# Cross-attention and mixture-of-experts block on one Trainium2 core: nine phases of two score slots in place of six of three, and the row maxima of two slots taken off in one pass

## The reference, cut to what matters

```python
q = latents @ Wq                       # latents = the 1024 rows of x, 8 heads of 64
k, v = split(concat([ctx, latents]) @ Wkv)
q = l2norm(q) * q_scale
k = l2norm(k) * k_scale
sim = einsum('bhid,bhjd->bhij', q, k) * 8
sim = where(mask, sim, -max)
attn = softmax(sim)                    # in float32
out = einsum('bhij,bhjd->bhid', attn, v)
x = x + layer_norm(out @ Wo)
x = x + shared_expert(ln(x)) + top2_of_16_experts(ln(x))
```

## Time and profile before

| | us |
|---|---|
| median of 3 runs | 801.37 (801.15 to 801.73) |
| the profiled execution, its own time | 803.27 |
| span of its profile | 801.5 |
| PE busy | 786.7 (98%) |
| DVE busy | 482.4 (60%) |
| POOL busy | 332.1 (41%) |
| ACT busy | 321.4 (40%) |
| maxima passes, L1001, 288 matmuls | 58.2 busy |

### The profile page before, as it was taken

The page is one execution under the profiler, slowest core; times in us unless marked ns, Lnnn a source line. Parts: engine busy times, 40 slices in busy tenths (PEclk is TensorE's granted clock), DMA queues, the critical chain, the costliest instruction groups (busy, mean ns, idle before and its releaser), DMA issues.

```text
span 801.5 us, 12996 instructions
## 1 busy us (share of the span) xinstructions
PE 786.7 (98%) x4358; PEld 483.7 (60%) x4359; DVE 482.4 (60%) x902; ACT 321.4 (40%) x499; POOL 332.1 (41%) x252
## 2 busy tenths in 40 slices
PE   8999999999999999999999989999999999999997
PEld 4444455554555545555554556656558999999554
DVE  3887777677786878686876855547123333333154
ACT  3455545555655556556554321121112333333110
POOL 2200045758586785858586133203560000000364
PEclk9999999999999999999999999999999999999999
DMA  3014800010001010000020112880522222222244
GB/s 119 27 36 152 262 23 1 1 28 1 28 1 29 0 29 2 20 9 2 27 66 28 27 30 76 267 267 38 184 96 62 93 92 92 92 92 79 79 131 125
DMA packets 53125, 56.39 MB, mean 70 GB/s; under 512 B 9290, under 2 KB 47700, under 8 KB 53076
## 3 DMA queue, kind: packets, MB, share of 16 engines
q1 hardware_dynamic: 49844, 47.23, 18.9%
q0 software_dynamic: 3072, 8.39, 3.2%
q10 hardware_dynamic: 160, 0.14, 0.0%
HBM read 36.73 MB, written 18.67 MB: 69 GB/s over the span
## 4 chain that ended last, share of the span: by engine, by line
PE 87%; issue 5%; POOL 3%; DVE 2%; DMA 1%; ACT 1%; POOLq 1%; DVEq 0%; SPq 0%; ACTq 0%
PE bank L1023 14%; PE score_banks L996 13%; PE score_banks L1248 11%; PE score_banks L1183 8%; PE score_banks L868 7%; PE bank L957 6%; PE bank L1257 5%; PE bank L1198 5%; PE score_banks L1001 4%; PE bank L868 4%; PE bank L941 2%; POOL slot_result L830 2%; PE bank L1183 2%; PE bank L1089 1%; PE score_banks L1238 1%
## 5 line engine op out<-in xcount | busy, mean ns | idle before, releaser
L1595 DVE TENSOR_REDUCE mx<-bank 128x1 f32<-128x512 f32 x248 | 159.3, 685 | 43.7 <-PE bank L957 42.6
L1371 ACT ACTIVATE prob<-score_banks,zero 128x1024 f32<-128x1024 f32 x128 | 142.6, 1116 | 85.3 <-PE score_banks L1001 78.7
L750 POOL TENSOR_TENSOR acc<-acc,prob 128x1024 f32<-128x1024 f32 (+1 forms) x67 | 160.6, 2397 | 22.2 <-DVE tail L1622 10.7
L1023 PE MATMUL bank<-prob,vn 128*64 128x512 f32 x512 | 121.1, 602 | 0.0
L830 POOL DMA_INDIRECT slot_result<-slot_results,posi x32 | 30.3, 947 | 163.8 <-DMA slot_results<-yo 148.9
L1183 PE MATMUL score_banks<-xfT,w12s 128*128 128x512 f32 x208 | 93.3, 593 | 0.8 <-ACT xfT L1432 0.8
L1248 PE MATMUL score_banks<-xsT,w_slot 128*128 128x128 f32 x752 | 91.9, 275 | 1.0 <-ACT xsT L1466 1.0
L1248 PEld LDWEIGHTS score_banks<-xsT,w_slot 128*128 128x128 f32 x752 | 89.2, 192 | 6.0 <-ACT xsT L1466 1.6
L742 POOL TENSOR_TENSOR acc<-prob 128x1024 f32<-128x1024 f32 x16 | 38.3, 2395 | 107.5 <-DVE on L1650 50.2
L1023 PEld LDWEIGHTS bank<-prob,vn 128*64 128x64 f32 x512 | 32.2, 136 | 58.2 <-issue 43.9
L1183 PEld LDWEIGHTS score_banks<-xfT,w12s 128*128 128x128 f32 x208 | 39.3, 190 | 40.8 <-issue 39.7
(11 more groups left out here) (200 smaller groups left out, 1126.6 us busy)
## 6 DMA issues: line engine op xcount, KB each, us to landing
w12r<-in_L_ffn_routed_w SPq DMA_DIRECT2D x32, 256.0 KB, 4.0
slot_rows<-zrow SPq DMA_DIRECT2D x47, 128.0 KB, 1.8
xsl<-slot_rows SPq DMA_DIRECT2D x47, 128.0 KB, 2.0
slot_results<-yo SPq DMA_DIRECT2D x47, 128.0 KB, 1.7
w3r<-in_L_ffn_routed_w SPq DMA_DIRECT2D x16, 256.0 KB, 3.1
rec<-row_sum_reciprocals SPq DMA_DIRECT2D x30, 128.0 KB, 2.9
xin<-in_x SPq DMA_DIRECT2D x16, 128.0 KB, 2.0
w12s<-in_L_ffn_shared_w SPq DMA_DIRECT2D x2, 1024.0 KB, 7.7
```

Source lines behind the costliest of these rows:

```text
L750: g.tensor_tensor(acc[rows, c, :, :], acc[rows, c, :, :], prob[rows, n % PROBS, :, :], ALU.add).then_inc(summed, 1)
L1023: last = mm_(o_bank(i, c)[rows, :], vn[:, kt, b, (2 * j + h) * DH:(2 * j + h + 1) * DH], prob[:, n % PROBS, h, :], start=(s == 0), stop=(s ...
L1371: a(prob[rows, held % PROBS, :, :], score_banks[n % 2][rows, :, :], ACT.Exp, bias=bias[rows, :])\
L1595: v.tensor_reduce(mx[:, h, t, c:c + 1], ring_bank(u)[:, :], AX.X, ALU.max).then_inc(ring_used, 1)
```

## The change

A pair's 18 slots now stand in nine phases of two. In each phase the first slot makes its three passes of products; then one pass of four matmuls with tiles of 32 rows x 128 columns takes the maxima of both slots off: two of them close the first slot's banks, the other two open the second slot's banks, whose three passes of products follow and close them (`take_maxima`, `score_slot(..., opened)`). For this the negated maxima stand twice in `neg_max`, at rows 0 to 31, 32 to 63, 64 to 95 and 96 to 127, each with its 8 tiles' rows; so `zneg` has a further axis, and `negate` has two reductions of the same size as the one before. The wait for `neg_max` at the start of a half stands before the maxima pass, as it did. The tables of turns and rounds are laid out anew over nine phases, the row sums of the previous pair move from the end of phase 0 to the end of phase 1, the other steps of DVE and ACT move to the phases that answer to theirs, and `weigh` is called twice a phase (once in phase 5) in place of three times. `PROBS` stays 6. In the last pair, a `weigh` that stood ahead of the third slot of the later phases goes back behind the slots.

```diff
--- before.py
+++ after.py
@@ -56,15 +56,16 @@
-BATCH = 3
+BATCH = 2
 RING = 3
+NEG_ROWS = P // 4
-SCORED = ((0, 1, 2), (3, 4, 5), (6, 7, 8), (9, 10, 11), (12, 13, 14), (15, 16, 17))
-WEIGHED = ((14, 15, 16), (0, 1, 2), (3, 4, 5), (6, 7, 8), (9, 10), (11, 12, 13))
+SCORED = ((0, 1), (2, 3), (4, 5), (6, 7), (8, 9), (10, 11), (12, 13), (14, 15), (16, 17))
+WEIGHED = ((15, 16), (0, 1), (2, 3), (4, 5), (6, 7), (8,), (9, 10), (11, 12), (13, 14))
 PHASES = len(SCORED)
-PROBS = 2 * BATCH
+PROBS = 3 * BATCH
...
-    zneg = sb("zneg", [P, 2, DH], stack=att)
+    zneg = sb("zneg", [P, 2, 2, NEG_ROWS], stack=att)
...
-    NEXT_TURNS = {(1, 3): (K_LEFT,), (3, 0): (Q_LEFT,), (3, 3): (K_RIGHT, K_CTX)}
-    OWN_ROUNDS = {0: ((), (8,), (9,), (10,)), 1: ((11,), (12,), (13,), ()), 2: ((14,), (15,), (RIGHT_MASKED,), ())}
-    NEXT_ROUNDS = {3: ((), (0,), (2,), ()), 4: ((4,), (6,), (1,), (3,)), 5: ((5,), (7,), (LEFT_MASKED,), ())}
+    NEXT_TURNS = {(2, 2): (K_LEFT,), (4, 0): (Q_LEFT,), (5, 2): (K_RIGHT,), (6, 2): (K_CTX,)}
+    OWN_ROUNDS = {0: ((), (8,), (9,)), 1: ((10,), (11,), (12,)), 2: ((13,), (14,), ()), 3: ((15,), (RIGHT_MASKED,), ())}
+    NEXT_ROUNDS = {4: ((), (0,), ()), 5: ((2,), (4,), ()), 6: ((6,), (1,), ()), 7: ((3,), (5,), ()),
+                   8: ((7,), (LEFT_MASKED,), ())}
...
-            if f == 0 and i:
+            if f == 1 and i:
                 ring_put("sums", i - 1)
...
-        for r in (0, DH):
+        for r in range(0, P, NEG_ROWS):
             g.affine_select(out=own_tile[:, :], in_=own_tile[:, :], compare_op=ALU.not_equal, fill=1.0,
...
+        def take_maxima(i, s, k, opens):
+
+            two = score_banks_of(i, s)
+            queries = score_place(s)[1]
+            for h in range(2):
+                at = slice((2 * k + h) * NEG_ROWS, (2 * k + h + 1) * NEG_ROWS)
+                last = mm_(two[h][:, :], ones_r[at, :], neg_max[at, queries], start=opens, stop=not opens,
+                           skip_group_check=True)
+                if not opens:
+                    last.then_inc(scores_made, 1)
+
-        def score_slot(i, s):
+        def score_slot(i, s, opened=False):
...
-            for lhs, rhs in ((k_hi[p], q_hi[p]), (k_hi[p], q_lo[p]), (k_lo[p], q_hi[p])):
+            for k, (lhs, rhs) in enumerate(((k_hi[p], q_hi[p]), (k_hi[p], q_lo[p]), (k_lo[p], q_hi[p]))):
                 for h, rows in enumerate((LOW, HIGH)):
-                    mm_(two[h][:, :], lhs[rows, keys], rhs[rows, queries], start=(lhs is k_hi[p] and rhs is q_hi[p]),
-                        stop=False)
-            if s in (0, BOTH + 1):
-                pe.wait_ge(ring_used, ring_freed("neg", i, c))
-            for h, rows in enumerate((LOW, HIGH)):
-                mm_(two[h][:, :], ones_r[rows, :], neg_max[rows, queries], start=False, stop=True)                    .then_inc(scores_made, 1)
+                    last = mm_(two[h][:, :], lhs[rows, keys], rhs[rows, queries], start=(k == 0 and not opened),
+                               stop=(k == 2 and opened), skip_group_check=True)
+                    if k == 2 and opened:
+                        last.then_inc(scores_made, 1)
...
                     if a < len(slots):
-                        score_slot(i, slots[a])
+                        score_slot(i, slots[a], a == 1)
+                        if a == 0 and f in NEG_AT:
+                            pe.wait_ge(ring_used, ring_freed("neg", i, NEG_AT[f]))
+                        if a != 1:
+                            take_maxima(i, slots[a], 0, False)
+                        if a == 0:
+                            take_maxima(i, slots[1], 1, True)
                 for one in weighed:
                     weigh(*one)
-                if f == 0 and i:
+                if f == 1 and i:
                     total_pair(i - 1)
...
-            v.tensor_reduce(zneg[:, :, tiles], mx[:, :, tiles, :], AX.X, ALU.max, negate=True).then_inc(neg_ready, 1)
+            v.tensor_reduce(zneg[:, 0, :, tiles], mx[:, :, tiles, :], AX.X, ALU.max, negate=True)
+            v.tensor_reduce(zneg[:, 1, :, tiles], mx[:, :, tiles, :], AX.X, ALU.max, negate=True).then_inc(neg_ready, 1)
...
-                if f == 2:
+                if f == 3:
                     negate(1)
                     add_two(i, 6, 0)
...
-                if f == 5 and more:
+                if f == 8 and more:
                     negate(0)
                     add_two(i, BOTH + 7, LEFT_SUMMED)
```

More of the change, by code:

```diff
@@ L376, in build @@
                 ring_put("o", i)
-            if f == 0 and i:
+            if f == 1 and i:
                 ring_put("sums", i - 1)
-            if i == PAIRS - 1 and f >= 3:
-                ring_put(*(("sum", NCH - 2), ("y", 0), ("y", 1))[f - 3])
+            if i == PAIRS - 1 and f in (5, 7, 8):
+                ring_put(*{5: ("sum", NCH - 2), 7: ("y", 0), 8: ("y", 1)}[f])
     ring_put("sum", NCH - 1)
@@ L681, in _ @@
             g.memset(buf[:, :], value)
-        g.memset(zneg[:, :, :], 0.0)
+        g.memset(zneg[:, :, :, :], 0.0)
         g.memset(ones_r[:, :].bitcast(F32), 1.0)
@@ L976, in turn_neg, with score_place, score_banks_of @@
             pe.wait_ge(neg_ready, 2 * i + z + 1)
-            nc.tensor.transpose(dst[:, 0:P], zneg[:, :, :].rearrange("p a d -> p (a d)"), ident[:, :])\
+            nc.tensor.transpose(dst[:, 0:P], zneg[:, :, :, :].rearrange("p k a d -> p (k a d)"), ident[:, :])\
                 .then_inc(ring_made, 1)
-        def score_slot(i, s):
+        def score_place(s):
+            c, kt = (0, s) if s <= BOTH else (1, TQ if s == BOTH + 1 else s - BOTH - 2)
+            return slice(kt * P, (kt + 1) * P), slice(c * QC, (c + 1) * QC)
+        def score_banks_of(i, s):
+            n = SLOTS * i + s
+            wait(pe, probs_ready, 2 * (n - 1))
+            return bank[2 * (n % 2)], bank[2 * (n % 2) + 1]
+        def take_maxima(i, s, k, opens):
[8 more added lines that the diff above has]
+        def score_slot(i, s, opened=False):
             p = i % 2
             n = SLOTS * i + s
-            two = bank[2 * (n % 2)], bank[2 * (n % 2) + 1]
-            wait(pe, probs_ready, 2 * (n - 1))
+            two = score_banks_of(i, s)
             if s == 0:
@@ L991, in score_slot @@
                 pe.wait_ge(v_used, late_count(TQ - 2))
-            c, kt = (0, s) if s <= BOTH else (1, TQ if s == BOTH + 1 else s - BOTH - 2)
-            keys, queries = slice(kt * P, (kt + 1) * P), slice(c * QC, (c + 1) * QC)
-            for lhs, rhs in ((k_hi[p], q_hi[p]), (k_hi[p], q_lo[p]), (k_lo[p], q_hi[p])):
+            keys, queries = score_place(s)
+            for k, (lhs, rhs) in enumerate(((k_hi[p], q_hi[p]), (k_hi[p], q_lo[p]), (k_lo[p], q_hi[p]))):
                 for h, rows in enumerate((LOW, HIGH)):
-                    mm_(two[h][:, :], lhs[rows, keys], rhs[rows, queries], start=(lhs is k_hi[p] and rhs is q_hi[p]),
-                        stop=False)
-            if s in (0, BOTH + 1):
-                pe.wait_ge(ring_used, ring_freed("neg", i, c))
-            for h, rows in enumerate((LOW, HIGH)):
-                mm_(two[h][:, :], ones_r[rows, :], neg_max[rows, queries], start=False, stop=True)                    .then_inc(scores_made, 1)
+                    last = mm_(two[h][:, :], lhs[rows, keys], rhs[rows, queries], start=(k == 0 and not opened),
+                               stop=(k == 2 and opened), skip_group_check=True)
+                    if k == 2 and opened:
+                        last.then_inc(scores_made, 1)
         def weigh(i, s):
@@ L1100, in stage_b @@
                 for a in range(len(slots) + 1):
-                    if not more and f >= PHASES // 2 and a == BATCH - 1:
-                        weigh(*weighed.pop(0))
                     for one in place_rounds(i, f, a):
@@ L1107, in stage_b @@
                     if a < len(slots):
-                        score_slot(i, slots[a])
+                        score_slot(i, slots[a], a == 1)
[5 more added lines that the diff above has]
+                            take_maxima(i, slots[1], 1, True)
                 for one in weighed:
                     weigh(*one)
-                if f == 0 and i:
+                if f == 1 and i:
                     total_pair(i - 1)
-                if not more and f == 3:
+                if not more and f == 5:
                     total(NCH - 2)
-                if not more and f > 3:
-                    project_o(f - 4)
+                if not more and f > 6:
+                    project_o(f - 7)
         for i in range(PAIRS):
@@ L1410, in stage_b @@
                     keep_o(i - 1, 1)
+                if f == 2 and i:
                     keep_sums(i - 1)
-                if f == 4 and i + 1 < PAIRS:
+                if f == 6 and i + 1 < PAIRS:
                     keep_o(i, 0)
@@ L1704, in stage_b @@
                 for a in range(len(slots) + 1):
-                    if f == 1 and a == BATCH and i:
+                    if f == 2 and a == BATCH and i:
```

(14 more changed lines are left out.)

## The result

The change made the kernel slower: 827.06 us, the median of four runs (826.33 to 829.18), against 801.55 (801.15 to 802.16) of the kernel before beside it. The ratio is 1.031, with a 95% interval of 1.0289 to 1.0332: 25.5 us. The forecast was 820.6, in a range of 806 to 840.

What follows compares the result with a forecast made beforehand. PE, busy 98%, was taken as the bound. Terms -16.6 + 14.4 + 7.2 + 6.0 + 1.6 + 4.5 - 2.4 + 4.5 gave +19.2 us, moving 801.4 to 820.6, range 806 to 840.

Steps and rivals of the forecast that it cites:

- Terms 1 to 3: Maxima passes on PE: 72 fewer save 16.6 us, shape-change edges add 14.4, weights that come late add 7.2.
- the row's 0.23: PE's maxima passes: four 32-row tiles run beside each other, so each pass takes 0.23 us as in the profile.
- term 6: Two rounds a pair at a third place come too soon for DVE; PE waits 0.28 us, 16 times: +4.5.
- Terms 4 and 5: Three more `weigh` groups a pair add 6.0 us; 20 rather than 18 costly first 64-row passes add 1.6.
- term 7: Rounds held to DVE's 1.30 us pace no longer wait where intervals lengthen to 1.55: half of 4.8 gained, -2.4.
- term 8: PE's wait for `neg_max` at the halves: DVE's sum meets POOL's, 0.3 us at each of 15 places, +4.5.
- Rival C: POOL stands in DVE's way at both halves, so the `neg_max` wait costs 34 us: 850 us, chance 0.08.
- term 4: Nine `weigh` groups a pair in place of six, 24 more in all, each adding edges and late weights: +6.0 us.
- costing nothing: Second `zneg` reduction, later row sums, and second-slot bank waits covered by `weigh` and products, phase 5 included: zero us.

Runs made afterwards that it cites:

- experiment 1: The kernel before, with its maxima passes in two tiles of 32 rows in place of 64: 842.4 us, 32.9 over the kernel before.
- experiment 2: The change with its nine phases, but two 64-row maxima matmuls for each slot: 825.8 us, 16.3 over the kernel before.
- experiments 3: The change with the right half of the next pair's keys turned in phase 4, not 5: 824.5 us, 15.0 over the kernel before.
- experiment 4: The change with 64-row maxima passes for each slot and the right keys turned in phase 4: 818.6 us, 9.0 over the kernel before.
- the change again: The change unaltered, measured once more on a second chip: 833.8 us, 24.9 over the kernel before.
- experiment 7: The change with 64-row maxima passes, right keys turned in phase 4, output projections a phase earlier: 818.7 us, 9.8 over the kernel before.
- Experiment 5: The change with the last pair's first two output projections a phase earlier: 832.8 us, against 833.8 for the change on the same chip.
- experiment 6: The kernel before, six phases kept, each phase's first two slots sharing a pass of four 32-row matmuls: 819.9 us, 10.9 over it.

## Why the prediction was right

It named the side and the main mechanism, and its range held the time; the likeliest value was 6.5 us too low. That it came so near is partly luck. A wait of 1.1 us in each of seven pairs (7.7 us) was not in the sum, and the last pair with what follows took 2.6 us more than was counted. Against that, the other terms were 0.7 a pair too high: 2.4 were forecast, and 2.8 less 1.1 are 1.7. By its terms:

- **Terms 1 to 3, the passes of four.** Expected edges of 0.10 on both sides and 0.10 for weights that aren't loaded ahead; the trace has 0.33 and 0.44 where 0.33 and 0.43 were written down. Four tiles ran beside each other: experiment 1's pass of two has the same 0.43 behind it. By the 3.07 times of the Trainium skill ("TensorE: Matmul & The Clock Gate", Part 3), which the prediction weighed, that would have been an estimated 0.50. The trace doesn't agree here, with 0.44 behind four tiles, and decides for the row's 0.23. Net cost of the passes in a kernel that has them: 0.7 us a pair by experiment 2, 0.8 by 3 against 4. Terms 1 to 3 alone give 0.6. But the waits of term 6 nearly vanish with 64-row passes too, so that they belong to this cost, and with them the forecast is 1.2: too high by some 0.4.
- **Terms 4 and 5, three more groups of `weigh`.** 7.6 us for eight pairs were expected, 5.2 with the gain of term 7. What is left in experiment 4 is 0.9 a pair, of which 0.3 is the wait of term 8: 0.6, or 5 for eight pairs. Term 7 was not measured by itself.
- **Term 6, rounds at a third place.** Expected 0.28, and PE does wait there: in the change's trace the last product pass starts at 291.53 and the round at 292.00, 0.47 later where 0.23 is plain:

```profile
291.53 0.40 PE L1018 MATMUL score_banks<-q_hi,k_lo 64*128 64x512 f32 x2
292.00 0.49 PE L959 MATMUL bank<-k_hi,q_hi 64*128 64x512 f32 x2
```

- **Term 8, the wait for `neg_max`.** Mis-sized, by chance on the high side: 0.3 was taken at each of 15 places. At the middle phase the chain ran as drawn:

```profile
308.27 0.40 PE L1018 MATMUL score_banks<-q_hi,k_lo 64*128 64x512 f32 x2
...
308.82 1.11 ACT L1395 ACTIVATE prob<-score_banks,zero 128x1024 f32<-128x1024 f32 x1 [0.35 <-PE score_banks L1018]
...
309.97 1.65 DVE L1648 TENSOR_TENSOR tail<-prob 128x1024 f32<-128x1024 f32 x1 [0.93 <-ACT prob L1395]
...
311.54 0.68 DVE L1639 TENSOR_TENSOR neg_max<-bank,own_tile 128x512 fp32r<-128x512 f32 x1
311.73 0.40 PE L1018 MATMUL score_banks<-q_hi,k_lo 64*128 64x512 f32 x2
...
312.27 0.51 PE L999 MATMUL score_banks<-neg_max,ones_r 32*128 32x512 f32 x4
```

DVE's sum took 1.65 and not 1.23, and the maxima pass started 0.54 after the last product in place of 0.33: 0.2 lost. At the start of the next pair in view, the third product stands at 289.97 and the pass at 290.30:

```profile
289.97 0.40 PE L1018 MATMUL score_banks<-q_hi,k_lo 64*128 64x512 f32 x2
290.30 0.50 PE L999 MATMUL score_banks<-neg_max,ones_r 32*128 32x512 f32 x4
```

Nothing is lost there. Over the whole trace the distance is 0.53 to 0.56 at six middle phases and 0.93 at the last pair's, and 0.33 elsewhere: about 2 us in all, where 4.5 were in the sum. Rival C, a whole POOL sum in the way at both halves, didn't come about. But the last pair shows what it would have cost: there the same place had 0.93 in this trace, 1.57 in that of the change again, and PE's wait of 2.35 us in experiment 7.
- **What failed: "The turned heads and maxima stay next to such groups in the new tables, so they add no shape changes" (term 4).** True of the shapes, and the wrong question for phase 5. The turn of the right keys had moved ahead of the one short `weigh` call of the pair, with an exponential, a rounding and a split queued between it and the ring bank that the next round wants. Under "costing nothing" phase 5 was looked at, but only for the exponentials. That is 1.1 us in each of seven pairs, 7.7 us, which experiments 3 and 4 take out with one table entry. It would have made the forecast some 828 with all else as it was.
- **The last pair** was taken as like the others. The turned maxima of its start stand in the two traces at these places, first before:

```profile
409.88 0.33 PE L977 MATMUL bank<-ident,zneg 128*128 128x128 f32 x1
```

And after:

```profile
428.81 0.33 PE L979 MATMUL bank<-ident,zneg 128*128 128x128 f32 x1
```

From there to the end of the span it is 391.6 and 396.6 us: 5.0 of the 23.9 arise in the last pair and behind it, 2.4 were in the sum. By the first product of the shared expert (L1183 before, at 467.45, and L1207 after, at 489.24) 2.9 of the 5.0 have arisen, 0.6 of them at `neg_max`, and the other 2.1 come later, outside the attention. Experiment 5 shows no gain from moving the projections. No other order of the last pair was tried, and what makes the rest stays open.

## What to carry to other kernels

Packing more tiles into a matmul pass saves that pass, but where its tile shape differs from its neighbours' it pays an edge on both sides and loads its weights in the open: here 0.30 us, more than a 512-column pass of 0.23. So a packed pass that is set alone into a stream of another shape doesn't pay. By the same prices it should pay where packed passes stand together, or beside a shape change that is there anyway; no run here shows that. And a step that is moved next to shorter work must be followed through every queue until it gives its buffer back, not only through the engine that issues it.

## What the runs showed of the hardware that was not expected

- A shape change costs the same 0.10 us a side for 64 to 32 rows as the earlier trace rows show for 64 to 128, and doesn't depend on the tiles in the pass: two or four 32-row matmuls have 0.33 ahead and 0.43 to 0.44 behind. An edit of one line, which changed only how many rows are read, cost 32.9 us.
- A pass fewer can cost time on another engine's account: with the second slot's own maxima pass gone, the round behind it came about 0.25 us late, held by DVE's reductions, in the change (0.47 in place of 0.23) and in experiment 6 (1.28 in place of 1.02) alike.
